# FFN input Hadamard-transformed on the activations, 256-token FFN tiles and one-bank PSUM work slots in a one-core attention + FFN kernel

## The reference, cut to what matters

```
x: [8, 512, 512]; per batch b (512 tokens):
  n   = layernorm(x)
  c_q = n @ W_dq + b_dq;  c_kv = n @ W_dkv + b_dkv          # 512 -> 128
  q = rotary(c_q @ W_qr + b_qr); k = rotary(n @ W_kr + b_kr)  # 16 heads of 32
  v = c_kv @ W_uv + b_uv
  x = x + layernorm(softmax(q k^T / sqrt(32)) v @ W_o + b_o)
  h   = fwht(layernorm(x) * SU_ug) / 64                     # Hadamard over 512
  up, gate = (h @ W_up^T) * 64 * ws_up, (h @ W_gate^T) * 64 * ws_gate   # 512 -> 2048
  h   = fwht(silu(gate) * up * SU_dp) / 64                  # Hadamard over 2048
  x = x + layernorm((h @ W_down^T) * 64 * ws_dp)            # 2048 -> 512
```

## Time and profile before

| | us |
|---|---|
| time, median of 3 runs (1955.82 to 1959.67) | 1959.06 |
| the profiled execution's own time | 1949.62 |
| its span, first to last instruction | 1947.8 |
| PE busy | 1853.1 (95%) |
| DVE busy | 1233.0 (63%) |
| ACT busy | 1087.2 (56%) |
| POOL busy | 936.4 (48%) |
| DMA, bytes moved | 281.06 MB |
| mean granted TensorE clock | 0.993 |

### The profile page before, as it was taken

One profiled execution on the slowest core, in us unless ns is written; L12 is line 12 of the kernel. 1 busy time (PEld: TensorE's weight loads), 2 busy tenths in 40 slices (PEclk: granted clock), 3 DMA queues, 4 the chain that ended last, 5 costly groups with the idle time before them and its releaser, 6 DMA issues.

```text
span 1947.8 us, 56765 instructions
## 1 busy us (share of the span) xinstructions
PE 1853.1 (95%) x24392; PEld 1371.0 (70%) x24392; DVE 1233.0 (63%) x2141; ACT 1087.2 (56%) x1731; POOL 936.4 (48%) x958
## 2 busy tenths in 40 slices
PE   3689989999999999999999999999999999999998
PEld 1366555777777776778677777777687877777786
DVE  7887666766677566766676667766676666654322
ACT  3566998565556564565556454655555555554222
POOL 3634554454455444644555445544555545434322
PEclk9899999999999999999999999999999999999999
DMA  8835423565456454665566544646566546543544
GB/s 242 255 108 148 126 56 82 137 163 142 131 129 180 115 131 129 174 159 129 149 159 164 126 126 135 169 123 149 140 164 154 136 131 146 149 126 125 172 149 147
DMA packets 353050, 281.06 MB, mean 144 GB/s; under 512 B 285216, under 2 KB 286496, under 8 KB 351776
## 3 DMA queue, kind: packets, MB, share of 16 engines
q1 hardware_dynamic: 343536, 265.83, 52.0%
q10 hardware_dynamic: 9264, 11.61, 2.1%
HBM read 189.30 MB, written 20.98 MB: 108 GB/s over the span
## 4 chain that ended last, share of the span: by engine, by line
PE 69%; DMA 7%; SPq 5%; ACT 5%; DVE 5%; POOL 5%; issue 3%; POOLq 0%; ACTq 0%; DVEq 0%
PE ps L855 26%; PE ps L879 12%; PE ps L797 5%; PE ps L785 5%; PE ps L809 4%; PE ps L825 4%; DMA qT<-tok 3%; PE ps L844 3%; PE ps L699 3%; SPq L605 3%; PE ps L830 2%; PE ps L751 2%; ACT pr L1029 2%; POOL pr L1450 1%; DMA xa<-in_x 1%
## 5 line engine op out<-in xcount | busy, mean ns | idle before, releaser
L1450 POOL TENSOR_TENSOR pr<-p,pr 128x512 f16<-128x512 f32 x256 | 296.9, 1160 | 329.2 <-ACT p L1035 329.2
L1029 ACT ACTIVATE pr<-ps,exp_scale 128x1024 f16<-128x1024 f32 x256 | 284.9, 1113 | 238.4 <-PE ps L809 174.9
L855 PE MATMUL ps<-x2T,gate_w 128*128 128x128 f16 x6144 | 385.0, 219 | 0.0
L855 PE MATMUL ps<-x2T,up_w 128*128 128x128 f16 x6144 | 385.0, 219 | 0.0
L855 PEld LDWEIGHTS ps<-x2T,gate_w 128*128 128x128 f16 x6144 | 359.6, 98 | 30.9 <-DVE room L1386 2.8
L855 PEld LDWEIGHTS ps<-x2T,up_w 128*128 128x128 f16 x6144 | 358.1, 98 | 23.5 <-issue 1.7
L1339 DVE TENSOR_REDUCE mx<-ps 128x2 f32<-128x1024 f32 x256 | 309.5, 1222 | 101.8 <-PE ps L797 100.6
L879 PE MATMUL ps<-room 128*128 128x512 f16 x1536 | 365.8, 379 | 6.0 <-DMA room<-down_mid 3.4
L1353 DVE TENSOR_TENSOR pr<-ps,pr 128x512 f16<-128x512 f32 x256 | 176.1, 688 | 297.4 <-ACT ps L1040 297.1
L1478 POOL TENSOR_TENSOR room<-room 128x256 f16<-128x256 f32 x256 | 171.9, 677 | 295.2 <-ACT room L1065 295.1
L879 PEld LDWEIGHTS ps<-room 128*128 128x128 f16 x1536 | 142.7, 98 | 161.1 <-issue 14.3
(11 more groups left out here) (191 smaller groups left out, 2414.9 us busy)
## 6 DMA issues: line engine op xcount, KB each, us to landing
room<-down_mid SPq DMA_DIRECT2D x256, 512.0 KB, 4.0
xr<-in_x SPq DMA_DIRECT2D x34, 256.0 KB, 3.9
y_mid<-xr SPq DMA_DIRECT2D x32, 256.0 KB, 4.1
room<-y_mid ACTq DMA_DIRECT2D x32, 256.0 KB, 3.4
xa<-in_x SPq DMA_DIRECT2D x30, 256.0 KB, 5.5
out<-room SPq DMA_DIRECT2D x24, 256.0 KB, 4.2
x2T<-in_W_gate SPq DMA_DIRECT2D x5, 1024.0 KB, 7.6
gate_w<-in_W_down SPq DMA_DIRECT2D x4, 1024.0 KB, 7.3
```

The lines of the kernel that those rows point to most:

```text
L855: mm = nc.tensor.matmul(ffn_ps[i % 2][:, col:col + P], weights[:, chunks[j // 4], kt, pw, j % 4 * P:(j % 4 + 1) * P], x2T[:, px, kt, t * P ...
L1029: nc.scalar.activation(pr[:, U % 2, 0].rearrange("p (j h) q -> p j (h q)", j=2), work[k], ACT.Exp, scale=exp_scale[:, 0:1]).then_inc(p_hi. ...
L1450: nc.gpsimd.tensor_tensor(lo, p32[:], hi, ALU.subtract).then_inc(p_low.sem, 1)
```

## The change

The Hadamard transform over 512 moves from the rows of W_up and W_gate to the FFN's input. DVE multiplies the centred y by SU_ug (`su`, a row held in SBUF) and does two butterfly levels across the four 128-column blocks (`yn`, now five instructions); ACT and DVE split it and apply the layernorm's factor (`yn`, `yw`; the remainder was POOL's); after `ln2` a new PE step `rot.t` multiplies by the 128 x 128 Hadamard matrix (2 matmuls with 512 columns), and ACT and DVE write the two halves back to `x2T`. `uh` is gone. W_up and W_gate are loaded once, in 16 pairs of row blocks, each with its own scale (`umx`: maximum of a pair; `ucut`; `ut`; `ue` straight to the merged tile `ug_w`); the scales are undone in `tanh` (`half_gate`, a column for each pair) and `gelu` (`h_scale`). W_down is loaded once too; two butterfly levels of its transform are done by POOL (`bf`, four additions of 1024 elements a chunk), so that `dz` has 2 matmuls and not 8.

The FFN works on 256 tokens: `gate.i`, `up.i` are 12 matmuls with 256 moving columns (one hidden block, two token tiles), `down.i` has its 6 matmuls for two tiles and sums into two banks, 7 and 3. Its weights come in 256 KB an iteration, into four buffers. `work` is three slots of one bank (0, 1, 2): `smax` and `st` are now one bank a step, `proj` and `v` likewise, and `exp` is two instructions of 512 columns. `pr` has three buffers in place of two. All lists are written anew.

```diff
-work = [ps[:, 0:2, :], ps[:, 2:4, :]]
+work = [ps[:, k, :] for k in range(3)]
-down_ps = ps[:, 7, :]
+down_ps = [ps[:, 7, :], ps[:, 3, :]]
...
 def dz(b, n):
-    pe.wait_ge(t_done, 4 * (n // 4) + 4)
-    mixed(n, n % 4)                       # 8 matmuls of 512 columns
+    pe.wait_ge(t_done, n + 1)
+    if n:
+        pe.wait_ge(q_done, n)
+    for i in range(2):
+        mm = nc.tensor.matmul(ps[:, 6, :], had[:], turned[n % 2][:, i, :], start=i == 0, stop=i == 1)
-def uh(b, n):
-    pe.wait_ge(t_done, 16 + 4 * (n // 4) + 4)
-    mixed(16 + n, n % 4)
...
+def rot(b, t):
+    k = slot(b, ("rot", t))
+    pe.wait_ge(*ln2_in.at(b, 16 * t + 15))
+    for i in range(2):
+        mm = nc.tensor.matmul(work[k], had[:], x2T[:, i, :, t * P:(t + 1) * P], start=i == 0, stop=i == 1)
+    mm.then_inc(rot_filled.sem, 1)
...
 def gate(b, i):
-    if i % (NJ // 2) == 0:
-        pe.wait_ge(*ln2_in.at(b, 16 * (i // (NJ // 2)) + 15))
+    if i % NJ == 0:
+        pe.wait_ge(*rot_done.at(b, 2 * (i // NJ) + 1))
...
 def down(b, i):
-    if jj == 0:
-        pe.wait_ge(*d_freed.at(b, t - 1))
+    if j == 0:
+        pe.wait_ge(*d_freed.at(b, 2 * tp - 1))
...
+def bf(b, k):                             # POOL
+    pool.wait_ge(d_in[k], 16)
+    for n, (src, dst, width) in enumerate(((d_raw[k], d_mid, 512), (d_mid, d_raw[k], 1024))):
...
+        nc.gpsimd.tensor_tensor(out_[:, :, 0, :], a_, b_, ALU.add)
+        nc.gpsimd.tensor_tensor(out_[:, :, 1, :], a_, b_, ALU.subtract).then_inc((d_turn, d_mixed)[n], 1)
...
 def fe(b, t):                             # ACT
-    sc.wait_ge(*fin_done.at(b, t - 1))
-    nc.scalar.activation(ft, down_ps, ...)
+    ot_free(fin_done.at(b, t))            # ot is shared with oe
+    nc.scalar.activation(ot[:], down_ps[t % 2], ...)
```

1019 lines of the change are left out of this document (559 added, 460 removed), and 4 rows, old and new, of the table MIDDLE.

## The result

| | before | after |
|---|---|---|
| time, median (range), us | 1959.37 (1955.82 to 1963.22) | 2045.62 (2043.93 to 2050.19) |
| ratio of the times | | 1.0443, 95% interval 1.0417 to 1.047 |
| the profiled execution's own time, us | 1949.62 | 2044.45 |
| its span, us | 1947.8 | 2042.7 |
| first `gate`, us | 347.9 | 401.0 |

The changed kernel is 4.4% slower, where 0.9% faster was forecast. The profiled execution after lies 111.9 us above the 1932.6 us of the sum: 73.1 us in the front (gate at 401.0, not 328), 38.8 us in the stretch behind (+41.8, not +3).

What follows compares the result with a forecast made beforehand. PE's stream was taken to bound everything behind the front, with DVE late next in the front. 1949.6 - 20 (front) - 2 (stream) + 2 (waits) + 3 (end) = 1932.6 us, scaled to a median of 1942; range 1912 to 1968 us.

Steps and rivals of the forecast that it cites:

- the sum: Over the whole kernel: the profiled execution's 1949.6 us with the forecast changes of front, stream, waits and end added, 1932.6 us.
- The butterflies' own price: Steady cycle, DVE: four butterfly instructions for each of 4 tiles, 0.41 us each, to 0.6 with semaphores.
- The last two tiles, +3 us: End of the kernel: two tiles finish together, adding one more statistics, ACT step and POOL addition, about +3 us.
- DVE at 92% (it has no long wait of its own to serve) gives 188 us: From first `exp` to first gate: DVE's 173 us of work at 92% busy takes 188 us, gate at 328.
- PE has 75 us less ahead of the first gate: Ahead of the first gate: PE loses 75 us of its 276, mainly the `uh` and most `dz` matmuls.
- 62 to 92% busy: Old front, 200 to 307 us: full granted clock at this PE load, argued against a slow-clock rival (1998 us, chance 0.05).
- My terms for ACT: Front: ACT's work ahead of the first `gelu` or `tanh` goes from 246 to about 230 us.
- a sign of being wrong: Front: a granted clock well under 1.00 between 140 and 320 us would show the forecast wrong.
- The start, forecast at +36: Start of the front: `bf` on POOL delays the first rotary sum to 79 us, first `exp` to about 140.
- the front gives nothing: Rival, front: the late start costs what PE gave; gate at 345 to 350 us, time of 1957 to 1964, chance 0.12.
- Against: in the cycle PE has no reason to wait for DVE at 158 of 213 us: Steady cycle: argument against a rival with new PE waits in every cycle, at 6 us about 1982 us, chance 0.13.
- the ring: Front, named after measuring: attention's `st`, `exp`, remainders on PE, ACT, DVE, each waiting for the next through PSUM slots.

Runs made afterwards that it cites:

- experiment 1: The changed kernel with the four butterfly instructions of `yn` on DVE left out: 2009.23 us, ratio 1.0277.
- experiment 11: The kernel before with `ut`, `uh`, `dy`, `dz` cut to one matmul each and the ACT and DVE steps emptying them to 128 columns: 1965.05 us, ratio 1.005.
- experiment 10: The changed kernel with the big weights' preparation cut to a skeleton on PE, DVE and ACT, all steps and semaphores kept: 2018.03 us, ratio 1.0309.
- experiment 12: The changed kernel with only DVE's and ACT's share of the weight preparation cut, PE's matmuls at full size: 2016.04 us, ratio 1.0326.
- experiment 3: The changed kernel with 456 matmuls that nobody reads put in PE's gaps from 240 to 400 us: 2036.98 us, ratio 1.0421.
- experiment 4: The changed kernel with POOL's `bf` additions on W_down cut to 8 elements each: 2027.74 us, ratio 1.0372.
- experiment 5: The changed kernel with `yn` cut in two and the front's lists reordered, first k and q ahead of the FFN weights: 2007.07 us, ratio 1.0269.
- experiment 2: The changed kernel with `yn` cut in two steps and one or two other steps put between: 2042.86 us, ratio 1.0451.
- experiment 7: The kernel before with four value-preserving DVE instructions of the butterflies' shapes added behind its `yn`: 2037.41 us, ratio 1.0423.

## Why the prediction was wrong

**Right.** A product is 1.31 us (the next group starts at 703.40 behind one at 702.09), as the earlier trace rows gave it and not as the 81 ns of the Trainium skill (TensorE: Matmul & The Clock Gate, section Back-to-back issue gap) would have, and PE's stream is as long as before: without the butterflies the cycle is 214.4 us (experiment 1). DVE's 158 us of a cycle (160.7 measured) and ACT's 130 (129.5). The butterflies' own price: 6.4 to 9.6 us of DVE a cycle foreseen, 10.2 measured, just above. The last two tiles, +3 us (2.6).

**The ledger of the front.** The gate stands 73 us behind the forecast: 18.8 us because the first `exp` came at 158.8 and not at 140, and 54.2 because the way from there to the gate took 242.2 us and not 188. The second is the larger error.

**"DVE at 92% (it has no long wait of its own to serve) gives 188 us": this step failed.** Behind the first `exp`, DVE had about as much work as computed (169.3 us busy, 173 foreseen), but it waited: 70% busy, not 92%. The waits from 148.9 us on show for whom: 46.6 us of ACT for `st`, 28.3 of DVE for `exr`. With it fell **"PE has 75 us less ahead of the first gate"**, of which I gave 20 us as the part that DVE would leave over. I took 92% busy for a sign that the front's length was PE's work. Experiment 11 took 72 us of busy time from PE in the kernel before and gained nothing, with the clock as the rival that it leaves. Experiments 10 and 12 say the same from the other side: with most of the preparation gone from DVE and ACT, 235 to 239 us are left.

**Readings of mine that were off.** I had PE busy for 214 of the 243 us from the first `st` to the gate, 88%; the trace of before gives 225.6, 93%. "62 to 92% busy" at full clock in 200 to 307 us is not in the rows, which give 92% for that stretch. My terms for ACT sum to 224 us and not 230 (231.3 measured). None of them moves the forecast much. The clock does more: I put PE at 122 us behind the first `exp` and said that a low clock costs little there; PE was busy for 173.9 us, at a granted clock of 0.80. I had named such a clock as a sign of being wrong. What it cost is known only net of added matmuls (experiments 3 and 12, 4 to 5 us).

**The start, forecast at +36, was +54.** Rotary sum 79 foreseen and 91.4 measured, first `dy` 116 and 130.9, first `exp` 140 and 158.8. I counted `bf` on POOL alone. Missing were DVE's list, which is as late (13 us, experiment 4), and what the two engines do to each other: two `ucut` at 2.58 and 3.36 us, not 1.2 to 1.4. And the start is paid in full (experiment 5: 35.5 us sooner, 35.0 at the gate). The rival "the front gives nothing" named the late start and stopped at the gain being lost. With no gain against it, it is a loss.

**"Against: in the cycle PE has no reason to wait for DVE at 158 of 213 us": the average again.** New waits of 0.3 us a cycle were forecast, bounds -1 and +3; it is 4.3. The rival gave them 0.13 and 6 us a cycle, and its size is near, but its mechanism is another: there `gate` waits for a late `rot`, or `down` for a bank. Here `rot` and `st` themselves wait for PSUM slots that `low` and the maxima behind `yn` give back late, and no wait for a `rot` stands among PE's longest. That its size is near is luck. I took DVE's average for its room; it is late at one place of its in-order list, and moving single steps there does not mend it (experiment 2). Experiment 7 shows that this needs no new slot or product: steps of the same shapes cost the old kernel 11.8 us a cycle. The end's +9.9 is 2.6 of mine and 7.3 of the same butterflies.

So the 94.9 us between the spans are: 53.7 late start, -0.6 from there to the gate, 31.6 in the seven cycles, 9.9 at the end, and 0.3 between `o.0` and the gate. Each is taken from the two traces; that of the first 36 us are order (16 are `bf`, by experiment 4, and the two overlap), and that most of the last ones are butterflies, is what experiments 1, 4 and 5 show.

**Open.** How long the ring takes by itself at full clock: in experiments 10 and 11 the clock fell with the work, and no run took work from PE and held the clock. Which of its links is the longest was read from waits only and not tried; a kernel with more PSUM slots in the front was not made. How much of the butterflies' 3.9 us a cycle is the port that DVE shares with POOL (it lengthens them by 4.9 us a batch), and how much their plain length (6.8 us), was not separated. And no version here beats the kernel before: the best, experiment 5, stays 2.7% behind it.

## What to carry to other kernels

Before a saving is counted, ask for a chain: an engine can be 92% busy and be hiding its work in another chain's gaps, and one at 66% can be full at the one place where it is waited for. Taking the work out of the old kernel (experiment 11) or putting the new work into it (experiment 7) gives both in one run each, before anything is rewritten. Look at the granted clock of such a run before it is read: work taken from TensorE can lower it.

A step put ahead of a kernel's first dependent sequence was paid in full here; the same steps moved behind it left the rest of the front as long as it was (experiment 5).

Steps given to GpSimd "because it is idle" are to be priced on VectorE too, where it has two inputs in SBUF at that time: here 1.28 us became 3.36.

## What the runs showed of the hardware that I had not expected

VectorE instructions with two SBUF inputs, while GpSimd adds tensors in SBUF: 1x512 in 2.87 and 2.73 us, with the additions gone 0.75 and 0.74; 128x1024 in 3.36 and 1.28; butterflies of 128x256 in 0.42 alone and mostly 1.26 to 1.43 beside a GpSimd addition, ending 0.28 us behind it. An instruction that takes one input from PSUM kept its 0.75 us in between (L1404 at 76.24). GpSimd's own additions went from 2.35 to as much as 3.34 us.

The granted TensorE clock was 0.98 over the front of the kernel before with PE 92% busy, 0.81 at 72%, 0.70 to 0.73 at 62 to 67%. Fillers brought it from 0.72 to 0.91. Fillers and matmuls put back (experiments 3 and 12) shortened the front by 4 to 5 us net, no more than such fronts scatter; the price of the clock alone was not measured.
